# Down projections in 128 and 48 rows: two gated cross-attention layers with mixtures of experts

## The chip, the cores and the metric

The kernel runs on one core of a Trainium2 chip. The metric is the device time in microseconds (us) of one execution: the median of 3 runs of the kernel before is 1052.2 us (1050.12 to 1055.38). One more execution was taken with the hardware profiler; all rows below come from it.

The core has TensorE (PE, with PEld for its weight loads), VectorE (DVE), ScalarE (ACT), GpSimd (POOL) and SyncE (SP), which issues most DMAs.

## What is computed

2048 tokens of 256 numbers go through two layers. Each layer is a cross-attention to a context of 512 rows, then a feed-forward part: a shared network of inner width 704, and a mixture of experts (8 experts, the best 2 for each token in layer 0; 16 experts, the best 4 in layer 1) of inner width 176. The part that matters here, cut from the reference:

```python
h = silu(x @ gate_w.T) * (x @ up_w.T)        # [tokens, 176] of an expert, [tokens, 704] of the shared one
acc = acc + w[:, None] * (h @ down_w.T)      # back to 256 columns
shared = silu(x @ sgate.T) * (x @ sup.T) @ sdown.T
```

## The kernel before

**High and low halves.** All products of f32 numbers are made from f16 pairs: a number is a high f16 and a low f16 (what the high one leaves). A product is three matmuls, high x high, high x low and low x high (`HL`). The helper `mm3` (line 261) issues them for `C` = 2 pieces of the contraction, so six matmuls for one result of 128 rows. Most matmuls of the kernel therefore have line L261 in the trace; they are told apart by tiles and shapes.

**Experts.** Tokens are sorted into slots; a tile of 128 slots belongs to one expert, a group is two tiles. There are 20 groups in layer 0 and 40 in layer 1 (`NG`). `group(base, s)` is one round of a software pipeline, written once for each engine and run in a hardware loop of four rounds a turn, with the first four and the last few unrolled. In round s PE does, in this order: the four transposes of the gathered rows of group s+1 (L753), the gate and up matmuls of group s (L261, tiles `region` and `wkh`, 12 matmuls of 352 columns), the four transposes of h of group s-1 (L782), and the down matmuls of group s-2 (L261, 12 matmuls of 256 columns). h of a tile has 176 columns; they are cut into two pieces of `EC` = 88, so the transposed h fills 88 partitions of one PSUM bank (bank 6), [88, 512] for two tiles and two pieces.

ACT in the same round makes the high half of the inputs of group s+1 (L830), silu of group s (L839) and the high half of the transposed h of group s-1 (L843). DVE makes the low half of the inputs (L910) and two small operations for the routing weight, the product h of group s (L926, twice), the low half of the transposed h of group s-1 (L932), and copies the result of group s-2 out of PSUM (L937). SP stores that result; POOL gathers the rows of a group four rounds ahead with two indirect DMAs (L663), and may issue them when h of an earlier group is made. In every case what PE takes from ACT and DVE was asked for a round before, except the result of a transpose, which is asked for two rounds ahead.

**Weights.** Weights come as f32 through four staging buffers (`stg`) and are split into high and low halves in `region` (experts) and `sgu`, `sdn` (shared). In layer 0 POOL does all splits (`split_on_pool`, L1584 to L1587); the layer 1 weights are split by POOL between its gathers in layer 0's expert stage, one of three parts after each group (`split_part`, L1468 to L1473), and by POOL and ACT during the attention (L1496 to L1505).

**Shared network.** The tokens are four blocks of 512; for each block the inner width is taken in six steps, five of 128 rows and a last one of 64 (`SREM`). A step is 12 gate/up matmuls of 512 columns (6 in the last step) and 12 down matmuls of 256 columns (L729, tiles `sdn` and `wkh`), the down matmuls two steps later. The first block runs beside the routing, before the experts; the other three run after them, beside DVE's combination of the experts' rows (L879), for which POOL gathers (L697).

Of the kernel before, what the change touches and what calls it, by code (L numbers as in the profile page):

```python
# [13 lines left out]
P = 128  # L14
D = 256
# [17 lines left out]
def gated_flamingo(nc, a, out):  # L33
# [8 lines left out]
    KT = CTX // P  # L42
    EI = a["dn0"].shape[1]
    EG = 2 * EI
    EC = EI // 2
    SI = a["sdn0"].shape[0]
    SG = 2 * SI
# [16 lines left out]
    with ExitStack() as ctx:  # L64
# [3 lines left out]
        def sem(name):  # L68
# [28 lines left out]
              region[:, 0:16 * 4 * EG].rearrange("p (e h c n) -> p e h c n", e=16, h=2, c=C))  # L97
        DN = (region[0:EC, half + 8 * 4 * EG:EXP_COLS].rearrange("p (e h c n) -> p e h c n", e=8, h=2, c=2),
              region[0:EC, 16 * 4 * EG:EXP_COLS].rearrange("p (e h c n) -> p e h c n", e=16, h=2, c=2))
        sgu = sb("sgu", [P, 2, C, SG], F16)  # L100
# [604 lines left out]
        def sums_ahead(l):  # L705

            return 2 if l == 1 else 1

        def ffn_pe(pe, l):
            def shared_gate_up(s):  # L710
# [8 lines left out]
            def shared_down(s):  # L719

                k, v = s % KSH, s % HR
                r = P if k < SFULL else SREM
                at_least(pe, s_hl[l], 0, s + 1)
                if k == 0:
                    at_least(pe, s_accr[l], 0, s // KSH + 1 - sums_ahead(l))
                first = shared_sums(l, s)
                for i in range(4):
                    for n, (h, j) in enumerate(HL):
                        last = nc.tensor.matmul(PS[:, first + i // 2, i % 2 * D:(i % 2 + 1) * D],  # L729
                                                wkh[0:r, HR * h + v, i * P:(i + 1) * P],  # L730
                                                sdn[0:r, j, k, :], start=(k == 0 and n == 0 and i % 2 == 0),
                                                stop=(k == KSH - 1 and n == 2), skip_group_check=True)
                last.then_inc(s_d[l].sem, 1)
# [30 lines left out]
            def group(base, s):  # L764
# [13 lines left out]
                if inside(base, s, 1, NG[l] + 1):  # L778
                    at_least(pe, e_h[l], base, s)
                    for n in range(2):  # L780
                        for c in range(C):
                            last = nc.tensor.transpose(PS[0:EC, 6, (2 * n + c) * P:(2 * n + c + 1) * P],  # L782
                                                       wk1[:, 3 - u, n * EI + c * EC:n * EI + (c + 1) * EC], idf[:, :])
                    last.then_inc(e_hT[l].sem, 1)
                if inside(base, s, 2, NG[l] + 2):
                    e = experts(base, s - 2)
                    at_least(pe, e_y[l], base, s - 2)
                    for n in range(2):
                        last = mm3(PS[:, 7, n * D:(n + 1) * D],
                                   lambda i, c: wkh[0:EC, 4 + 2 * u + i, (2 * n + c) * P:(2 * n + c + 1) * P],  # L790
                                   lambda h, c: DN[l][:, bass.ds(e[n], 1), h, c, :].rearrange("p o n -> p (o n)"))
                    last.then_inc(e_d[l].sem, 1)
# [13 lines left out]
        def ffn_act(act, l):  # L806
# [25 lines left out]
            def group(base, s):  # L832
# [8 lines left out]
                if inside(base, s, 1, NG[l] + 1):  # L841
                    at_least(act, e_hT[l], base, s)
                    nc.scalar.activation(wkh[0:EC, 6 - 2 * u, :], PS[0:EC, 6, :], ACT.Copy).then_inc(e_hh[l].sem, 1)  # L843
            at_least(act, s_d[l], 0, HALF)
# [11 lines left out]
        def ffn_dve(dve, l):  # L856
# [36 lines left out]
            def shared_low(s):  # L893
                u, r = s % 2, (P if s % KSH < SFULL else SREM)
                at_least(dve, s_hh[l], 0, s + 1)
                at_least(dve, s_d[l], 0, s + 1 - HR)
                nc.vector.tensor_tensor(wkh[0:r, HR + s % HR, :], wk1[0:r, 2 + u, :], wkh[0:r, s % HR, :],  # L897
                                        ALU.subtract).then_inc(s_hl[l].sem, 1)
# [20 lines left out]
            def group(base, s):  # L919
# [508 lines left out]
        items += gu1[:GU_EARLY]  # L1428
        items += [(EC, a["dn1"][e].rearrange("(c p) n -> p c n", c=2), DN[1][:, e, 0], DN[1][:, e, 1]) for e in range(E[1])]
        items += gu1[GU_EARLY:]  # L1430
# [9 lines left out]
        items.append((SREM, a["sdn1"][SFULL * P:, :].unsqueeze(1), sdn[0:SREM, 0, SFULL:SFULL + 1, :], sdn[0:SREM, 1, SFULL:SFULL + 1, :]))  # L1440
        ROUNDS0 = 2 + E[0] // 2
# [75 lines left out]
        def _(sp):  # L1517
# [73 lines left out]
        def split_layer0(pl):  # L1591
# [15 lines left out]
        def split_experts0(pl, first, end):  # L1607
            for e in range(first, end):
# [3 lines left out]
                split_on_pool(pl, 2 * k + 1, seen, 2 * D, DN[0][:, e, 0].rearrange("p c n -> p (c n)"),  # L1612
                              DN[0][:, e, 1].rearrange("p c n -> p (c n)"), EC)
            if end == E[0]:
# [521 lines left out]
def laid_out(inputs):  # L2136

    import numpy as np
    v = {k: np.asarray(a) for k, a in inputs.items()}
    n = {}  # L2140
    n["x"] = v["x"].reshape(-1, v["x"].shape[-1])
# [5 lines left out]
    n["gu0"] = np.concatenate([v["L0_ffn_w_gate"], v["L0_ffn_w_up"]], 2)  # L2147
    n["dn0"] = v["L0_ffn_w_down"]
    n["gu1"] = np.concatenate([v["L1_ffn_gate_w"].transpose(0, 2, 1), v["L1_ffn_up_w"].transpose(0, 2, 1)], 2)
    n["dn1"] = v["L1_ffn_down_w"].transpose(0, 2, 1)  # L2150
    for l, (g, u, d) in enumerate(((v["L0_ffn_sw_gate"], v["L0_ffn_sw_up"], v["L0_ffn_sw_down"]),
                                   (v["L1_ffn_shared_gate_w"].T, v["L1_ffn_shared_up_w"].T, v["L1_ffn_shared_down_w"].T))):
        cuts = range(0, g.shape[1], 128)
        n[f"sgu{l}"] = np.concatenate([w[:, c:c + 128] for c in cuts for w in (g, u)], 1)
        n[f"sdn{l}"] = d
    n["g_xattn"], n["g_ffn"] = v["g_xattn"], v["g_ffn"]
# [21 lines left out]
```

## Time and profile before

| | |
|---|---|
| median of 3 runs | 1052.2 us (1050.12 to 1055.38) |
| span of the profiled execution | 1057.0 us, the only time known of it |
| mean granted TensorE clock | 0.824 of 2.4 GHz |
| PE, DVE, POOL, ACT busy | 859.4, 747.4, 627.5, 471.7 us |
| layer 0: first shared block, experts, rest of the shared network | about 150 to 190, 190 to 281, 281 to 360 us |
| layer 1 attention | about 360 to 700 us |
| layer 1: routing and first shared block, experts, rest | about 700 to 760, 761 to 946, 946 to 1057 us |

An instruction's row has its start, its duration, its engine and line (L12 is line 12 of the kernel), the tiles it writes and reads, and its shape. For matmuls `88*128` is the shape of the stationary tile, rows times columns, and `128x256` what comes out. The duration of a matmul includes its way through the array, so successive ones overlap; their pace is read from the differences of starts. The time in square brackets is what the engine was idle before the row and what ended it.

### The profile page before, as it was taken

How to read it: one execution, taken by the hardware profiler on the slowest of the kernel's cores; microseconds unless marked ns; L12 is line 12 of the kernel's file. 1: busy time of each engine (PE TensorE's matmuls, PEld its weight loads, DVE VectorE, ACT ScalarE, POOL GpSimd, SP SyncE). 2: the span in 40 equal slices, each digit the busy share in tenths (PEclk: the TensorE clock that was granted, in tenths of full speed). 3: DMA queues.
4: the chain of work that ended last, by engine and by line, in shares of the span. 5: the costliest groups of instructions: out<-in, count | busy, mean ns of one | idle time of the engine just before them, and what ended most of it. 6: DMA issues, size and time to landing. Idle time of an engine off the chain costs nothing.

```text
span 1057.0 us, 21171 instructions
## 1 busy us (share of the span) xinstructions
PE 859.4 (81%) x6928; PEld 579.0 (55%) x6929; DVE 747.4 (71%) x1624; ACT 471.7 (45%) x1018; POOL 627.5 (59%) x830
## 2 busy tenths in 40 slices
PE   4489668799988879887887787858699999879585
PEld 2267545577645446555555555544567788645243
DVE  5788768466566788898798888958666777536255
ACT  3455344233222368767667767734133334213111
POOL 4587882766284868878778788710244444624670
PEclk8689869899999955667668668868799999969787
DMA  7021242345231231121110100020134444432331
GB/s 255 21 83 29 62 133 60 111 137 151 98 109 49 81 130 38 62 95 43 61 43 15 29 26 4 2 71 16 33 108 130 126 140 133 136 96 71 104 95 50
DMA packets 65766, 85.55 MB, mean 81 GB/s; under 512 B 11148, under 2 KB 56976, under 8 KB 65680
## 3 DMA queue, kind: packets, MB, share of 16 engines
q1 hardware_dynamic: 55312, 55.30, 16.0%
q0 software_dynamic: 10368, 29.14, 10.4%
q8 instruction: 48, 0.79, 0.3%
q14 instruction: 38, 0.31, 0.1%
HBM read 61.93 MB, written 32.98 MB: 90 GB/s over the span
## 4 chain that ended last, share of the span: by engine, by line
PE 43%; DVE 16%; POOL 12%; issue 11%; POOLq 5%; DVEq 4%; ACT 4%; another core or an unknown queue 3%; DMA 2%; SPq 0%; ACTq 0%
PE PS L261 25%; PE PS L729 4%; DVE sb_slotv L1364 4%; POOL sb_xnf L663 3%; PE PS L753 2%; PE PS L782 2%; PE PS L1245 2%; DVE sb_wkh L1369 2%; PE PS L1235 1%; PE PS L370 1%; DMA sb_x_sb<-x 1%; PE PS L268 1%; PE PS L397 1%; POOL sb_wk L1703 1%
## 5 line engine op out<-in xcount | busy, mean ns | idle before, releaser
L261 PE MATMUL PS<-sb_region,sb_wkh 88*128 (+1 forms) x1440 | 213.4, 299 | 13.0 <-issue 9.4
L663 POOL DMA_INDIRECT sb_xnf<-token_table,sb_ids x120 | 115.9, 966 | 166.6 <-DVE sb_ids L577 75.0
L1364 DVE TENSOR_REDUCE sb_slotv<-PS 128x1 f32<-128x512 f32 x256 | 163.7, 681 | 26.5 <-PE PS L1235 26.5
L261 PEld LDWEIGHTS PS<-sb_region,sb_wkh 88*128 88x128 f16 (+1 forms) x1440 | 140.6, 100 | 63.3 <-issue 18.8
L261 PE MATMUL PS<-sb_xnT,sb_sgu 128*128 128x512 f16 x528 | 136.3, 407 | 12.7 <-issue 11.9
L811 ACT ACTIVATE sb_wk<-PS 128x512 f32<-128x512 f32 (+1 forms) x48 | 28.6, 595 | 172.2 <-PE PS L261 131.4
L1319 ACT ACTIVATE sb_wk<-PS,sb_slotv 128x512 f32<-128x512 f32 x128 | 87.1, 690 | 23.8 <-DVE sb_slotv L1364 23.5
L261 PEld LDWEIGHTS PS<-sb_xnT,sb_sgu 128*128 128x128 f16 x528 | 53.0, 103 | 80.5 <-issue 33.2
L729 PE MATMUL PS<-sb_sdn,sb_wkh 128*128 128x256 f16 (+1 forms) x576 | 76.5, 284 | 22.1 <-DVE sb_wkh L897 13.5
L1703 POOL TENSOR_SCALAR sb_wk<-sb_wk 128x512 f32<-128x512 f32 x128 | 79.4, 620 | 16.6 <-ACT sb_wk L1319 7.1
L890 DVE SCALAR_TENSOR_TENSOR sb_wk<-PS,sb_wk 128x512 f32<-128x512 f32 (+1 forms) x48 | 33.2, 692 | 70.1 <-ACT sb_wk L811 56.3
L1369 DVE TENSOR_SCALAR sb_wkh<-PS 128x1024 f16<-128x1024 f16 x112 | 76.6, 684 | 8.4 <-PE PS L1257 8.4
L729 PEld LDWEIGHTS PS<-sb_sdn,sb_wkh 128*128 128x128 f16 (+1 forms) x576 | 56.4, 101 | 46.2 <-DVE sb_wkh L897 20.9
L926 DVE SCALAR_TENSOR_TENSOR sb_wk<-PS,sb_sm,sb_wk 128x176 f32<-128x176 f32 x120 | 42.6, 397 | 53.8 <-ACT sb_wk L839 47.0
L830 ACT ACTIVATE sb_wkh<-PS 128x512 f16<-128x512 f32 x60 | 35.8, 596 | 99.2 <-PE PS L753 67.2
L697 POOL DMA_INDIRECT sb_xnf<-slot_table,sb_place x48 | 46.8, 976 | 45.6 <-DMA slot_table<-sb_wa 17.1
L839 ACT ACTIVATE sb_wk<-PS 128x352 f32<-128x352 f32 x60 | 27.8, 463 | 89.8 <-PE PS L261 82.1
L910 DVE TENSOR_TENSOR sb_wkh<-PS,sb_wkh 128x512 f16<-128x512 f32 x60 | 41.4, 690 | 32.7 <-ACT sb_wkh L830 23.1
L1319 ACT ACTIVATE sb_wkh<-PS,sb_slotv 128x512 f32<-128x512 f32 x64 | 43.4, 683 | 33.6 <-DVE sb_slotv L1364 23.3
L753 PE MATMUL PS<-sb_idf,sb_xnf 128*128 128x128 f32 x240 | 39.4, 287 | 18.9 <-DMA sb_xnf<-token_table,sb_ids 16.9
L1245 PE MATMUL PS<-sb_idh,sb_wk 128*128 128x128 f16 x512 | 53.5, 264 | 1.2 <-POOL sb_wk L1703 0.7
L1245 PEld LDWEIGHTS PS<-sb_idh,sb_wk 128*128 128x128 f16 x512 | 38.9, 119 | 24.8 <-issue 22.7
(292 smaller groups left out, 1883.4 us busy)
## 6 DMA issues: line engine op xcount, KB each, us to landing
slot_table<-sb_wa SPq DMA_DIRECT2D x60, 256.0 KB
slot_table<-token_table SPq DMA_DIRECT2D x16, 640.0 KB
sb_stg<-gu SPq DMA_DIRECT2D x24, 352.0 KB, 3.0
sb_stg<-dn SPq DMA_DIRECT2D x24, 176.0 KB
token_table<-sb_xnf SPq DMA_DIRECT2D x16, 256.0 KB, 3.9
sb_stg<-sgu SPq DMA_DIRECT2D x8, 352.0 KB, 6.6
sb_x_sb<-x SPq DMA_DIRECT2D x1, 2048.0 KB, 12.1
out<-sb_x_sb SPq DMA_DIRECT2D x16, 128.0 KB
```

The lines of the kernel that those rows point to most:

```text
L261: last = nc.tensor.matmul(out_, lhs(i, c), rhs(j, c), start=(c == 0 and n == 0 and not begun), stop=(c == C - 1 and n == 2 and not more))
L663: nc.gpsimd.indirect_dma_start(xg[l][:, 2 * (g % XR) + n, :], None, xw[l][:, :], bass.IndirectOffsetOnAxis(ap=ids[:, 2 * g + n:2 * g + n + ...
L697: nc.gpsimd.indirect_dma_start(yr[l][r][:, k, :], None, ys[l][:, :], bass.IndirectOffsetOnAxis(ap=place[:, k, t:t + 1], axis=0))\
L729: last = nc.tensor.matmul(PS[:, first + i // 2, i % 2 * D:(i % 2 + 1) * D], wkh[0:r, HR * h + v, i * P:(i + 1) * P], sdn[0:r, j, k, :], st ...
L753: last = nc.tensor.transpose(PS[:, 4 + s % 2, (2 * n + c) * P:(2 * n + c + 1) * P], xg[l][:, 2 * (s % XR) + n, c * P:(c + 1) * P], idf[:, :])
L910: nc.vector.tensor_tensor(wkh[:, 2 * (s % 2) + 1, :], PS[:, 4 + s % 2, :], wkh[:, 2 * (s % 2), :], ALU.subtract).then_inc(e_xl[l].sem, 1)
L926: last = nc.vector.scalar_tensor_tensor(wk1[:, 2 + u, n * EI:(n + 1) * EI], PS[:, 2 * u + n, EI:EG], wv[u][:, n:n + 1], wk1[:, u, n * EI:( ...
L1245: last = nc.tensor.transpose(bank[:, (h * KT + k) * P:(h * KT + k + 1) * P], h_p[s % NE][:, h, k * P:(k + 1) * P], idh[:, :])
L1319: nc.scalar.activation(h_e[s % NE][:, h, :], PS[:, 2 * u + h, :], ACT.Exp, bias=h_nb[u][:, h:h + 1], accum_out=o_sum[v][:, head:head + 1]) ...
L1364: nc.vector.tensor_reduce(h_nb[u][:, h:h + 1], PS[:, 2 * u + h, :], AX, ALU.max, negate=True).then_inc(h_max, 1)
L1369: nc.vector.tensor_scalar(h_T[s % 2], PS[:, 4 + s % 2, :].bitcast(F16), -RB, None, ALU.add).then_inc(h_pc_dve, 1)
L1703: nc.gpsimd.tensor_scalar(h_e[s % NE][:, h], h_e[s % NE][:, h], 255.0, MAGIC + RB_BITS, ALU.mult, ALU.add).then_inc(h_int, 1)
```

## The change

The 176 inner columns of h are cut into 128 and 48 (`EREM`) instead of 88 and 88. The first piece needs three matmuls as before. Of the second, the high half is written to partitions 0 to 47 and the low half to partitions 64 to 111 of the same tile, and the down weights of this piece are laid out twice, at rows 0 to 47 and 64 to 111 with zeros between. One matmul over 112 rows then gives high x high and low x high, one more over the 48 high rows gives high x low weights: five matmuls in place of six for each tile (`DOWN_PARTS`). The transposes of h make [128, 128] and [48, 128] results, ACT's copy and DVE's subtraction become two instructions each, and a memset clears the partitions between 48 and 64. The shared network's last 64 rows are treated the same way: their low half goes to partitions 64 to 127, `sdn`'s last rows are laid out twice, and its last step has two matmuls in place of three for each of four results. The host lays the weights out (`down_parts`); DMAs and splits of these weights now have 128 rows.

```diff
+        LOW_AT = P // 2
+        DOWN_PARTS = ((P, 0, 0, 0), (P, 0, 0, 1), (P, 1, 0, 0), (LOW_AT + EREM, 0, 1, 0), (EREM, 0, 1, 1))
...
                 for i in range(4):
-                    for n, (h, j) in enumerate(HL):
+                    for n, (h, j) in enumerate(HL if k < SFULL else HL[:2]):
+                        r = P if k < SFULL or n == 0 else SREM
                         last = nc.tensor.matmul(PS[:, first + i // 2, i % 2 * D:(i % 2 + 1) * D],
                                                 wkh[0:r, HR * h + v, i * P:(i + 1) * P],
...
                     for n in range(2):
                         for c in range(C):
-                            last = nc.tensor.transpose(PS[0:EC, 6, (2 * n + c) * P:(2 * n + c + 1) * P],
-                                                       wk1[:, 3 - u, n * EI + c * EC:n * EI + (c + 1) * EC], idf[:, :])
+                            r = P if c == 0 else EREM
+                            last = nc.tensor.transpose(PS[0:r, 6, (2 * c + n) * P:(2 * c + n + 1) * P],
+                                                       wk1[:, 3 - u, n * EI + c * P:n * EI + c * P + r], idf[:, :])
...
                     for n in range(2):
-                        last = mm3(PS[:, 7, n * D:(n + 1) * D],
-                                   lambda i, c: wkh[0:EC, 4 + 2 * u + i, (2 * n + c) * P:(2 * n + c + 1) * P],
-                                   lambda h, c: DN[l][:, bass.ds(e[n], 1), h, c, :].rearrange("p o n -> p (o n)"))
+                        for p, (r, i, c, h) in enumerate(DOWN_PARTS):
+                            last = nc.tensor.matmul(PS[:, 7, n * D:(n + 1) * D],
+                                                    wkh[0:r, 4 + 2 * u + i, (2 * c + n) * P:(2 * c + n + 1) * P],
+                                                    DN[l][0:r, bass.ds(e[n], 1), h, c, :].rearrange("p o n -> p (o n)"),
+                                                    start=(p == 0), stop=(p == len(DOWN_PARTS) - 1))
...
-                    nc.scalar.activation(wkh[0:EC, 6 - 2 * u, :], PS[0:EC, 6, :], ACT.Copy).then_inc(e_hh[l].sem, 1)
+                    nc.scalar.activation(wkh[:, 6 - 2 * u, 0:2 * P], PS[:, 6, 0:2 * P], ACT.Copy)
+                    nc.scalar.activation(wkh[0:EREM, 6 - 2 * u, 2 * P:4 * P], PS[0:EREM, 6, 2 * P:4 * P],
+                                         ACT.Copy).then_inc(e_hh[l].sem, 1)
...
-                nc.vector.tensor_tensor(wkh[0:r, HR + s % HR, :], wk1[0:r, 2 + u, :], wkh[0:r, s % HR, :],
+                low = wkh[:, HR + s % HR, :] if r == P else wkh[SREM:2 * SREM, s % HR, :]
+                nc.vector.tensor_tensor(low, wk1[0:r, 2 + u, :], wkh[0:r, s % HR, :],
                                         ALU.subtract).then_inc(s_hl[l].sem, 1)
...
-                    nc.vector.tensor_tensor(wkh[0:EC, 7 - 2 * u, :], PS[0:EC, 6, :], wkh[0:EC, 6 - 2 * u, :],
-                                            ALU.subtract).then_inc(e_hl[l].sem, 1)
+                    nc.vector.tensor_tensor(wkh[:, 7 - 2 * u, 0:2 * P], PS[:, 6, 0:2 * P], wkh[:, 6 - 2 * u, 0:2 * P],
+                                            ALU.subtract)
+                    nc.vector.tensor_tensor(wkh[LOW_AT:LOW_AT + EREM, 6 - 2 * u, 2 * P:4 * P], PS[0:EREM, 6, 2 * P:4 * P],
+                                            wkh[0:EREM, 6 - 2 * u, 2 * P:4 * P], ALU.subtract).then_inc(e_hl[l].sem, 1)
...
+            nc.vector.memset(wkh[LOW_AT - 32:LOW_AT, 4::2, 2 * P:4 * P], 0.0)
             dve.drain()
...
-                    load(2 * k + 1, (base, 2 + s), de.rearrange("(c p) n -> p c n", c=2), 2 * D, EC)
+                    load(2 * k + 1, (base, 2 + s), de.rearrange("(c p) n -> p c n", c=2), 2 * D)
...
-            split_on_pool(pl, 3, 32, D, sdn[0:SREM, 0, SFULL, :], sdn[0:SREM, 1, SFULL, :], SREM)
+            split_on_pool(pl, 3, 32, D, sdn[:, 0, SFULL, :], sdn[:, 1, SFULL, :])
...
+    def down_parts(w):
+
+        rest = w[:, 128:]
+        gap = np.zeros((w.shape[0], 64 - rest.shape[1], w.shape[2]), w.dtype)
+        return np.concatenate([w[:, 0:128], rest, gap, rest, gap], 1)
```

## Rows read from the trace of the kernel before

**Rows 1.** The page: engines' busy time, and the chain by line.
```profile
PE 859.4 (81%) x6928; PEld 579.0 (55%) x6929; DVE 747.4 (71%) x1624; ACT 471.7 (45%) x1018; POOL 627.5 (59%) x830
...
PE PS L261 25%; PE PS L729 4%; DVE sb_slotv L1364 4%; POOL sb_xnf L663 3%; PE PS L753 2%; PE PS L782 2%; PE PS L1245 2%; DVE sb_wkh L1369 2%; PE PS L1235 1%; PE PS L370 1%; DMA sb_x_sb<-x 1%; PE PS L268 1%; PE PS L397 1%; POOL sb_wk L1703 1
```

**Rows 2.** Windows: busy us (x) of PE, PEld, DVE, ACT, POOL; granted clock; DMA share, GB/s.
```profile
191.00:281.00 90.00, 84.26 (x634) 64.29 (x633) 56.60 (x136) 31.32 (x59) 51.60 (x52) 0.96 0.44 130
771.00:915.00 144.00, 141.63 (x1120) 111.39 (x1119) 102.17 (x246) 55.52 (x106) 68.36 (x75) 1.00 0.45 131
```

**Rows 3.** The timeline, PE alone, one round of layer 1's experts.
```profile
863.49 0.60 PE L753 MATMUL PS<-sb_idf,sb_xnf 128*128 128x128 f32 x4
863.93 1.95 PE L261 MATMUL PS<-sb_region,sb_wkh 128*128 x12
865.72 0.60 PE L782 MATMUL PS<-sb_idf,sb_wk 128*88 128x128 f32 x4
866.15 1.48 PE L261 MATMUL PS<-sb_region,sb_wkh 88*128 x12
867.47 0.60 PE L753 MATMUL PS<-sb_idf,sb_xnf 128*128 128x128 f32 x4
```

**Rows 4.** The chain that ended last, 183 to 282 us: shares by line, and splits.
```profile
by line: POOL sb_xnf L663 25.6%; issue 21.0%; PE PS L261 20.3%; DMA sb_xnf<-token_table,sb_ids 6.8%; POOL sb_region L1473 6.1%; POOLq L1472 5.1%; POOL sb_stg L1470 3.1%; POOL sb_region L1468 3.1%; PE PS L753 2.7%; PE PS L782 2.4%; DVE sb_wk
...
200.81 1.52 POOL sb_region L1473
...
213.71 1.52 POOL sb_region L1473
```

**Rows 5.** The timeline, PE alone, layer 0's experts, where it waited.
```profile
207.50 0.90 PE L753 MATMUL PS<-sb_idf,sb_xnf 128*128 128x128 f32 x4 [2.24 <-DMA sb_xnf<-token_table,sb_ids]
208.45 3.29 PE L261 MATMUL PS<-sb_region,sb_wkh 128*128 x12
...
234.24 0.66 PE L753 MATMUL PS<-sb_idf,sb_xnf 128*128 128x128 f32 x4 [0.86 <-DMA sb_xnf<-token_table,sb_ids]
```

**Rows 6.** The timeline, PE alone, shared steps of layer 1.
```profile
968.85 2.75 PE L261 MATMUL PS<-sb_xnT,sb_sgu 128*128 128x512 f16 x12
971.44 1.47 PE L729 MATMUL PS<-sb_sdn,sb_wkh 128*128 128x256 f16 x12
972.75 2.75 PE L261 MATMUL PS<-sb_xnT,sb_sgu 128*128 128x512 f16 x12
975.44 1.48 PE L729 MATMUL PS<-sb_sdn,sb_wkh 64*128 64x256 f16 x12
976.85 2.76 PE L261 MATMUL PS<-sb_xnT,sb_sgu 128*128 128x512 f16 x12
```

**Rows 7.** The timeline, weight loads alone, at the same step.
```profile
975.43 0.55 PEld L729 LDWEIGHTS PS<-sb_sdn,sb_wkh 64*128 64x128 f16 x6 [0.42 <-issue]
```

**Rows 8.** The timeline, PE alone, bias rows of one row.
```profile
54.47 0.39 PE L268 MATMUL PS<-sb_lg,sb_ones_h 1*128 1x256 f16 x2
54.79 0.83 PE L261 MATMUL PS<-sb_wa,sb_wkh 128*128 128x256 f16 x6
55.55 0.39 PE L268 MATMUL PS<-sb_lg,sb_ones_h 1*128 1x256 f16 x2
```

**Rows 9.** Groups by line and shape: count, busy us, mean ns, idle before.
```profile
L843 ACT ACTIVATE sb_wkh<-PS 88x512 f16<-88x512 f32 x60 | 35.4, 590 | 9.4 <-PE PS L782 7.5 <-remote 1.7
L839 ACT ACTIVATE sb_wk<-PS 128x352 f32<-128x352 f32 x60 | 27.8, 463 | 89.8 <-PE PS L261 82.1 <-issue 5.4 <-remote 2.4
L926 DVE SCALAR_TENSOR_TENSOR sb_wk<-PS,sb_sm,sb_wk 128x176 f32<-128x176 f32 x120 | 42.6, 397 | 53.8 <-ACT sb_wk L839 47.0 <-issue 6.7
L932 DVE TENSOR_TENSOR sb_wkh<-PS,sb_wkh 88x512 f16<-88x512 f32 x60 | 40.8, 679 | 5.8 <-ACT sb_wkh L843 2.8 <-issue 2.4
```

**Rows 10.** The same view, POOL alone, low halves of weights.
```profile
L1505 POOL TENSOR_TENSOR sb_region<-sb_stg,sb_region 88x512 f16<-88x512 f32 x14 | 16.1, 1151 | 2.3 <-issue 2.3
L1505 POOL TENSOR_TENSOR sb_sdn<-sb_stg,sb_sdn 128x512 f16<-128x512 f32 x2 | 2.3, 1156 | 0.3 <-issue 0.3
```

More of the change, by code:

```diff
@@ L42, in gated_flamingo @@
     KT = CTX // P
[L43 to L46, printed above, removed]
+    EG = a["gu0"].shape[2]
+    EI = EG // 2
+    EREM = EI - P
+    SI = a["sgu0"].shape[1] // 2
     SG = 2 * SI
@@ L97, in gated_flamingo @@
               region[:, 0:16 * 4 * EG].rearrange("p (e h c n) -> p e h c n", e=16, h=2, c=C))
-        DN = (region[0:EC, half + 8 * 4 * EG:EXP_COLS].rearrange("p (e h c n) -> p e h c n", e=8, h=2, c=2),
-              region[0:EC, 16 * 4 * EG:EXP_COLS].rearrange("p (e h c n) -> p e h c n", e=16, h=2, c=2))
+        DN = (region[:, half + 8 * 4 * EG:EXP_COLS].rearrange("p (e h c n) -> p e h c n", e=8, h=2, c=2),
+              region[:, 16 * 4 * EG:EXP_COLS].rearrange("p (e h c n) -> p e h c n", e=16, h=2, c=2))
         sgu = sb("sgu", [P, 2, C, SG], F16)
@@ L721, in shared_down @@
                 k, v = s % KSH, s % HR
-                r = P if k < SFULL else SREM
                 at_least(pe, s_hl[l], 0, s + 1)
@@ L731, in shared_down @@
                                                 sdn[0:r, j, k, :], start=(k == 0 and n == 0 and i % 2 == 0),
-                                                stop=(k == KSH - 1 and n == 2), skip_group_check=True)
+                                                stop=(k == KSH - 1 and n == 1), skip_group_check=True)
                 last.then_inc(s_d[l].sem, 1)
@@ L1428, in gated_flamingo @@
         items += gu1[:GU_EARLY]
-        items += [(EC, a["dn1"][e].rearrange("(c p) n -> p c n", c=2), DN[1][:, e, 0], DN[1][:, e, 1]) for e in range(E[1])]
+        items += [(P, a["dn1"][e].rearrange("(c p) n -> p c n", c=2), DN[1][:, e, 0], DN[1][:, e, 1]) for e in range(E[1])]
         items += gu1[GU_EARLY:]
@@ L1439, in gated_flamingo @@
             items.append((P, g[:, cs, :], sdn[:, 0, cs, :], sdn[:, 1, cs, :]))
-        items.append((SREM, a["sdn1"][SFULL * P:, :].unsqueeze(1), sdn[0:SREM, 0, SFULL:SFULL + 1, :], sdn[0:SREM, 1, SFULL:SFULL + 1, :]))
+        items.append((P, a["sdn1"][SFULL * P:, :].unsqueeze(1), sdn[:, 0, SFULL:SFULL + 1, :], sdn[:, 1, SFULL:SFULL + 1, :]))
         ROUNDS0 = 2 + E[0] // 2
@@ L1552, in _ @@
                 load(n, (0, 1), d[:, cs, :], (cs.stop - cs.start) * D)
-            load(3, (0, 1), a["sdn0"][SFULL * P:, :].unsqueeze(1), D, SREM)
+            load(3, (0, 1), a["sdn0"][SFULL * P:, :].unsqueeze(1), D)
             def two_experts(base, s):
@@ L1612, in split_experts0 @@
                 split_on_pool(pl, 2 * k + 1, seen, 2 * D, DN[0][:, e, 0].rearrange("p c n -> p (c n)"),
-                              DN[0][:, e, 1].rearrange("p c n -> p (c n)"), EC)
+                              DN[0][:, e, 1].rearrange("p c n -> p (c n)"))
             if end == E[0]:
@@ L2147, in laid_out @@
     n["gu0"] = np.concatenate([v["L0_ffn_w_gate"], v["L0_ffn_w_up"]], 2)
-    n["dn0"] = v["L0_ffn_w_down"]
+    n["dn0"] = down_parts(v["L0_ffn_w_down"])
     n["gu1"] = np.concatenate([v["L1_ffn_gate_w"].transpose(0, 2, 1), v["L1_ffn_up_w"].transpose(0, 2, 1)], 2)
-    n["dn1"] = v["L1_ffn_down_w"].transpose(0, 2, 1)
+    n["dn1"] = down_parts(v["L1_ffn_down_w"].transpose(0, 2, 1))
     for l, (g, u, d) in enumerate(((v["L0_ffn_sw_gate"], v["L0_ffn_sw_up"], v["L0_ffn_sw_down"]),
@@ L2154, in laid_out @@
         n[f"sgu{l}"] = np.concatenate([w[:, c:c + 128] for c in cuts for w in (g, u)], 1)
-        n[f"sdn{l}"] = d
+        n[f"sdn{l}"] = np.concatenate([d, d[len(d) // 128 * 128:]], 0)
     n["g_xattn"], n["g_ffn"] = v["g_xattn"], v["g_ffn"]
```

## The prediction, made before the change was built or run

> **What bounds the kernel now.** I read the page's busy shares and its chain first. PE is busy 81% of the span and its matmul line L261 alone is 25% of the chain, but POOL, DVE and idle "issue" time hold much of the rest [rows 1]. So the change has to be priced stage by stage, and I went to the table of windows for the two expert stages. In layer 1's (771 to 915 us) PE is busy 141.6 of 144 us at full granted clock, DVE 102, POOL 68 and ACT 56 [rows 2]: PE sets the pace. In layer 0's (191 to 281 us) PE is busy 84 of 90 us.
>
> The timeline of PE in layer 1 shows one round [rows 3]: four input transposes (L753) from 863.49, twelve gate/up matmuls from 863.93, four h transposes (L782) from 865.72, twelve down matmuls (88 rows) from 866.15, the next transposes at 867.47. That is 0.44 + 1.79 + 0.43 + 1.32 = 3.98 us, nothing between them. A down matmul costs 1.31 / 12 = 0.109 us, a transpose the same. Everything else in a round depends on the round before, so what PE needs per round is what the stage costs, forty times.
>
> Layer 0's twenty rounds are different. The chain there is mostly POOL's gathers and weight splits [rows 4]. POOL serves three groups from one L1473 to the next, 213.71 - 200.81 = 12.9 us on the shortest turn: 4.30 us a group, 0.3 more than PE's 3.98. PE therefore stands waiting for gathers three times, 3.9 us in all; the first two stand in [rows 5], 2.24 and 0.86.
>
> **What the change takes away.** Each group has 10 down matmuls in place of 12: 2 x 0.109 = 0.22 us a round. The shared network's last step of each block of 512 tokens has 8 matmuls in place of 12: 0.44 us, four blocks in each layer. The down matmuls with 88 rows and the shared ones with 128 both start 0.109 us apart [rows 3, 6], so filling the rows costs nothing by itself.
>
> **What it adds on PE.** The shapes now alternate. Of the ten down matmuls the fifth and the tenth have a stationary tile of 48 rows, the others of 128 or 112. Of the four h transposes the second and the fourth have 48 columns (the loop still runs n outside, c inside). In a shared last step 128 and 64 rows alternate four times. The trace has such a border: the shared step with 64 rows, between steps with 128 [rows 6]. The gate/up matmuls ahead of it take 975.44 - 972.75 = 2.69 us, where those ahead of a 128-row step take 971.44 - 968.85 = 2.59; the 64-row step itself takes 976.85 - 975.44 = 1.41 us, where a 128-row one takes 1.31. So entering costs 0.10 us and leaving costs 0.10 us. The weight-load row says how: the first load of the 64-row tile comes after 0.42 us without one [rows 7], while loads otherwise run ahead of the matmuls. Bias rows of one row show the same: two matmuls take 54.79 - 54.47 = 0.32 us in place of 0.22, and six matmuls after them 0.76 in place of 0.65 [rows 8]. 88 rows pay nothing, 64 and 1 row pay; 48 lies between the two that pay, so I count 48 rows as paying.
>
> The Trainium skill, "TensorEngine Tiling (Array Packing)", section "Key Properties", says that changing the tiling mode, not just the tile, drains TensorE; its list of row modes steps from 128 to 64 to 32 rows. The trace agrees for rows, with 0.10 us each way. By this rule the change trades 0.22 us of matmuls for the borders.
>
> Down matmuls: into and out of 48 rows twice, 4 x 0.10 = 0.40, less 0.22: +0.18 us a round. Transposes: into and out of 48 columns twice. No row of the trace has fewer than 88 columns, so the price of a column border is bounded from below by 0 (88 columns pay nothing) and from above by 0.10 plus a doubled transpose. I take 0.10, the price of the only change of shape the trace shows: 4 x 0.10 = +0.40 us. Together a round costs 3.98 + 0.58 = 4.56 us.
>
> **What it adds elsewhere.** ACT's copy of h becomes two. 352 columns take 0.463 us and 512 take 0.590 [rows 9], 0.8 ns a column, so two of 256 take about 0.78: +0.19. DVE's subtraction becomes two: by its 176-column and 512-column rows (0.397 and 0.679 us), 0.46 each, +0.25 at most. DVE is busy 2.8 us of a 3.98 us round and ACT 1.5 [rows 2], and PE asks for the result one round later, so both are hidden; only where the pipeline empties at a layer's end do they show, some 0.35 us twice, 0.7 in all. If PE were not the bound they would cost 0.2 each a round. POOL's splits run over 128 rows in place of 88 at the same 512 columns: 1151 ns with 88 rows, 1156 with 128 [rows 10]: nothing, and so for the shared last rows. The loads of down weights grow from 176 to 256 KB; they are issued ahead and POOL stands between their landing and their use, nothing, and 0.5 us each on the few first ones if not. One memset of DVE per layer falls where DVE waits for gathers: nothing, else 0.4. Its new waits: none; the semaphore of each pair is on the second instruction.
>
> **The sum.** Layer 1: of 40 rounds, 36 lie in the full stretch (144 / 3.98), the others where the pipeline fills and empties and PE waits in part, which absorbs some. I take 38 x 0.58 = 22.0 us (34 to 40 rounds: 19.7 to 23.2). Layer 0: 20 x 0.58 = 11.6, but with 4.56 us PE is now slower than POOL's 4.30, so the three waits (3.9 us) go and with them most of the half-clock group behind the first (3.29 in place of 1.95 us [rows 5], 1.3): +6.4 (5 to 11.6). Shared last steps: six more borders, 0.60, less 0.44: +0.16, eight times: +1.3 (0 to 1.5). Ends: +0.7. In all +30.4 us. The profiled execution has a span of 1057.0 us, 4.8 over the median of the runs, 1052.2; it goes to 1087, the median to **1082**. With the bounds, and some 3 us for the stages behind, where work meets other work when it is shifted, this case by itself gives 1072 to 1093.
>
> **Rivals.**
> *Column borders are free.* Speaks for it: nothing in the trace shows one. Then a round costs +0.18: 38 x 0.18 = 6.8, in layer 0 the round of 4.16 stays under POOL's 4.30 and half of 3.6 shows, 1.8; with the shared steps and ends 10.6: 1063.
> *The 48-column transposes also get slower themselves.* A 128-column f32 transpose takes 0.109 us, twice what 128 f16 columns could take at the rate of 256 in 0.109 [rows 3, 6]; f32 goes at half rate already, and if a narrow tile halves it once more, two of four transposes double: +0.22 a round, 58 times, 12.7 us: 1095. The Trainium skill, "TensorEngine Tiling (Array Packing)", section "Restrictions", lists the f32 transpose mode among what column tiling disables; no row here shows it.
> *No borders at all: faster.* If tiles of 48 rows and of 48 columns are handled as the 88-row ones are, the change does what it removes: -0.22 x 38 = -8.3 in layer 1; in layer 0 PE carries the chain in only some 9 rounds, -2.0; the shared steps -0.44 x 8 = -3.5 if 64-row matmuls too alternate freely; ends +0.7: 1039. The deciding point is whether a border costs over 0.22 / 4 = 0.055 us in the down part. The 64-row and 1-row rows speak against it.
> *DVE becomes the bound* would need its 2.8 us plus 0.25 to pass PE's round; it doesn't in any case above.
>
> **How the numbers follow.** Borders on both: 0.62. Columns free: 0.14. Slower transposes as well: 0.11. No borders: 0.10. The 0.03 left is a net of nothing. The predicted time is the first case's, 1082. The range goes from 1058 (columns free, with some cover) to 1098; it leaves out the case without borders and little above. Half a per cent is 5.3 us, about what a measurement can tell from no change: faster 0.10, same 0.04, slower 0.86.
>
> **What would show it.** In layer 1 the round should be 4.56 us: gate/up still 1.79, the h transposes 0.8 in place of 0.43, the down part 1.5 in place of 1.32. Matmuls of 48 rows should start about 0.2 us after the one before and be followed after 0.2. In layer 0 the waits of PE for gathers should be gone. A round of 4.16 with transposes at 0.43 would mean free columns; one of 3.76 would overturn the argument; one near 4.8 would mean slower transposes. PE idle between rounds, waiting for DVE or ACT, would mean that the cover failed.

## The result, and the profile after

The changed kernel takes 1058.17 us, median of 20 runs (1054.2 to 1065.17), where the kernel before, run beside it, takes 1051.77 (1046.4 to 1057.88, 20 runs). The ratio is 1.0064, 95% interval 1.0043 to 1.0084: slower by 6.4 us, where 30 had been forecast. The span of its profiled execution is 1059.6 us. Medians here and below are of all runs; the ratios leave out the slow ones, those over 1.5% above the fastest run of the same kernel.

The page: busy time by engine, and the chain that ended last by line (L794 are the down matmuls of the experts, L732 those of the shared network, L756 and L786 the transposes).

```profile
PE 868.5 (82%) x6776; PEld 558.3 (53%) x6777; DVE 761.1 (72%) x1686; ACT 475.0 (45%) x1078; POOL 630.3 (59%) x830
...
PE PS L261 20%; PE PS L794 7%; DVE sb_slotv L1376 4%; PE PS L732 4%; PE PS L756 3%; PE PS L786 2%; PE PS L1257 2%; DVE sb_wkh L1381 2%; PE PS L1247 1%; POOL sb_xnf L663 1%; PE PS L370 1%; POOL sb_wk L1715 1%; DMA sb_x_sb<-x 1%; PE PS L268 1%
```

Against [rows 1], PE has 152 matmuls fewer (6928 to 6776) and is busy 9 us more: fewer, but dearer. The same windows as [rows 2] (busy us and count of PE, PEld, DVE, ACT, POOL; granted clock; DMA share; GB/s):

```profile
191.00:281.00 90.00, 84.73 (x576) 56.96 (x576) 61.29 (x155) 32.29 (x78) 54.25 (x55) 0.96 0.43 130
771.00:915.00 144.00, 142.28 (x995) 97.21 (x994) 103.58 (x268) 54.48 (x134) 64.57 (x69) 0.98 0.41 123
```

In layer 1 PE is still busy nearly all the time (142.3 of 144 us), and DVE is no nearer to being the bound (103.6 of 144 us, 102.2 before). One round of this stage, the timeline of PE alone and then of its weight loads:

```profile
863.90 0.66 PE L756 MATMUL PS<-sb_idf,sb_xnf 128*128 128x128 f32 x4
864.39 1.95 PE L261 MATMUL PS<-sb_region,sb_wkh 128*128 x12
866.18 0.60 PE L786 MATMUL PS<-sb_idf,sb_wk 128*128 128x128 f32 x4
866.62 1.57 PE L794 MATMUL PS<-sb_region,sb_wkh 128*128 x10
868.12 0.66 PE L756 MATMUL PS<-sb_idf,sb_xnf 128*128 128x128 f32 x4
```

```profile
866.04 0.47 PEld L786 LDWEIGHTS PS<-sb_idf,sb_wk 128*128 128x128 f32 x4
866.51 0.43 PEld L794 LDWEIGHTS PS<-sb_region,sb_wkh 128*128 128x128 f16 x4
867.15 0.54 PEld L794 LDWEIGHTS PS<-sb_region,sb_wkh 48*128 48x128 f16 x5 [0.21 <-issue]
867.91 0.09 PEld L794 LDWEIGHTS PS<-sb_region,sb_wkh 48*128 48x128 f16 x1 [0.21 <-issue]
868.12 0.42 PEld L756 LDWEIGHTS PS<-sb_idf,sb_xnf 128*128 128x128 f32 x4
```

Against [rows 3] the parts stand so: input transposes 0.49 (0.44), gate and up 1.79 (1.79), h transposes 0.44 (0.43), down 1.50 (1.32). The round is 868.12 - 863.90 = 4.22 us, where 3.98 became 4.56 in the forecast. The h transposes, two of which now have 48 columns, take what they took. The loss is in the down part and in the step behind it (+0.18 and +0.05), beside the tiles of 48 rows. The load rows show where: in front of each of the two 48-row loads there is a hole of 0.21 us in which nothing is loaded, as there was one of 0.42 at the 64-row tile of [rows 7]; and the load for the next transposes comes at the time of their first matmul, 868.12, while the one for the h transposes is ahead of it (866.04 and 866.18).

The shared network's last step, the timeline of PE, to be held against [rows 6]:

```profile
978.78 1.47 PE L732 MATMUL PS<-sb_sdn,sb_wkh 128*128 128x256 f16 x12
980.09 2.75 PE L261 MATMUL PS<-sb_xnT,sb_sgu 128*128 128x512 f16 x12
982.68 1.77 PE L732 MATMUL PS<-sb_sdn,sb_wkh 128*128 128x256 f16 x8
984.38 2.76 PE L261 MATMUL PS<-sb_xnT,sb_sgu 128*128 128x512 f16 x12
```

Eight matmuls take 984.38 - 982.68 = 1.70 us, where twelve took 1.41; the gate and up matmuls before them take 2.59 in place of 2.69, for the first tile behind them now has 128 rows. Together that is +0.19 us a block.

ACT's two copies of the transposed h and DVE's two subtractions (by line and shape: count, busy us, mean ns, idle before), the rows that answer to L843 and L932 of [rows 9]:

```profile
L849 ACT ACTIVATE sb_wkh<-PS 128x256 f16<-128x256 f32 x60 | 23.0, 383 | 6.0 <-PE PS L786 2.7 <-remote 1.7 <-issue 1.6
L850 ACT ACTIVATE sb_wkh<-PS 48x256 f16<-48x256 f32 x60 | 21.9, 365 | 0.0
L943 DVE TENSOR_TENSOR sb_wkh<-PS,sb_wkh 48x256 f16<-48x256 f32 x60 | 25.1, 418 | 0.8
L941 DVE TENSOR_TENSOR sb_wkh<-PS,sb_wkh 128x256 f16<-128x256 f32 x60 | 24.9, 415 | 3.2 <-issue 2.3 <-ACT sb_wkh L850 0.7
```

0.75 us in place of 0.59, and 0.83 in place of 0.68: +0.16 and +0.15, both hidden in the round.

What is left to explain: 40 + 20 rounds at +0.24 and eight blocks at +0.19 are 15.9 us if nothing absorbs them, and the kernel lost 6.4. Besides, the last stage of the profiled executions (from the second shared gate/up matmuls to the last shared down matmul) is 97.5 us long after, and 104.7 before, as if the change gave 7 us back there.

### The profile page after: what moved, and what is told of

Its sections match the earlier page's. It is cut to its first block, busy times and chain, and to the rows that moved or that the text cites. A ratio compares the mean times of both kernels' runs of the same rounds, so it can differ in the third digit from the quotient of the medians.

```text
span 1059.6 us, 20989 instructions
## 1 busy us (share of the span) xinstructions
PE 868.5 (82%) x6776; PEld 558.3 (53%) x6777; DVE 761.1 (72%) x1686; ACT 475.0 (45%) x1078; POOL 630.3 (59%) x830
## 4 chain that ended last, share of the span: by engine, by line
PE 46%; DVE 15%; POOL 10%; issue 10%; POOLq 5%; DVEq 4%; ACT 4%; another core or an unknown queue 4%; DMA 2%; SPq 0%; ACTq 0%
PE PS L261 20%; PE PS L794 7%; DVE sb_slotv L1376 4%; PE PS L732 4%; PE PS L756 3%; PE PS L786 2%; PE PS L1257 2%; DVE sb_wkh L1381 2%; PE PS L1247 1%; POOL sb_xnf L663 1%; PE PS L370 1%; POOL sb_wk L1715 1%; DMA sb_x_sb<-x 1%; PE PS L268 1%
## 5 line engine op out<-in xcount | busy, mean ns | idle before, releaser
L261 PE MATMUL PS<-sb_xnT,sb_sgu 128*128 128x512 f16 x528 | 130.8, 397 | 7.9 <-issue 7.2
L261 PE MATMUL PS<-sb_region,sb_wkh 128*128 x720 | 123.2, 321 | 7.9 <-issue 7.8
L794 PE MATMUL PS<-sb_region,sb_wkh 128*128 x600 | 95.0, 277 | 4.4 <-DVE sb_wa L948 4.1
L732 PE MATMUL PS<-sb_sdn,sb_wkh 128*128 128x256 f16 (+1 forms) x544 | 77.0, 283 | 24.7 <-DVE sb_wkh L906 15.0
L261 PEld LDWEIGHTS PS<-sb_region,sb_wkh 128*128 128x128 f16 x720 | 71.7, 100 | 44.6 <-issue 10.7
L732 PEld LDWEIGHTS PS<-sb_sdn,sb_wkh 128*128 128x128 f16 (+1 forms) x544 | 53.3, 100 | 52.1 <-DVE sb_wkh L906 21.8
L794 PEld LDWEIGHTS PS<-sb_region,sb_wkh 128*128 128x128 f16 x600 | 52.6, 97 | 43.2 <-issue 32.1
L756 PE MATMUL PS<-sb_idf,sb_xnf 128*128 128x128 f32 x240 | 41.4, 298 | 15.3 <-DMA sb_xnf<-token_table,sb_ids 15.3
```

The costliest lines, as they stand in the source:

```text
L261: last = nc.tensor.matmul(out_, lhs(i, c), rhs(j, c), start=(c == 0 and n == 0 and not begun), stop=(c == C - 1 and n == 2 and not more))
L756: last = nc.tensor.transpose(PS[:, 4 + s % 2, (2 * n + c) * P:(2 * n + c + 1) * P], xg[l][:, 2 * (s % XR) + n, c * P:(c + 1) * P], idf[:, :])
L794: last = nc.tensor.matmul(PS[:, 7, n * D:(n + 1) * D], wkh[0:r, 4 + 2 * u + i, (2 * c + n) * P:(2 * c + n + 1) * P], DN[l][0:r, bass.ds(e[ ...
```

## The experiments

**Full rows.** The last down matmul of a tile goes over 112 rows like the one before it, and that of the shared network over 128. The weights are laid out twice anyway, so this adds the product low x low of the short piece, which all the other sums leave out; it takes nothing away. No tile of fewer than 112 rows is left. The column widths of the h transposes still alternate.

```diff
-        DOWN_PARTS = ((P, 0, 0, 0), (P, 0, 0, 1), (P, 1, 0, 0), (LOW_AT + EREM, 0, 1, 0), (EREM, 0, 1, 1))
+        DOWN_PARTS = ((P, 0, 0, 0), (P, 0, 0, 1), (P, 1, 0, 0), (LOW_AT + EREM, 0, 1, 0), (LOW_AT + EREM, 0, 1, 1))
...
-                        r = P if k < SFULL or n == 0 else SREM
+                        r = P
```

> The changed kernel with the last matmul of the down product, and the last of the shared step, over all rows of their stationary tile (112 and 128 in place of 48 and 64): the same number of matmuls, no matmul with 48 rows left, and 64-row tiles only where the kernel before the change has them outside these steps. The products added are low x low, so the sum is the same product, a little more exact. Theory: the cost is the borders between tiles of 128 and of 64 rows, and they alone. Then a round of layer 1's experts goes from 4.22 to 3.98 - 0.22 = 3.76 us, the expert stage of layer 1 is 38 x 0.22 = 8 us shorter than before the change and 18 us shorter than with it, and the kernel is 5 to 12 us faster than before the change. Rival: the cost is in the doubled copies of ACT and DVE, or in the weights' layout: the round stays at 4.2 us. Second rival: DVE becomes the bound: a round of 3.9 or more with PE waiting for DVE.

Measured: 1042.81 us (1039.84 to 1044.71, 6 runs) beside 1054.7 of the kernel before (23 runs); ratio 0.9896, interval 0.9855 to 0.9936. The timeline of PE:

```profile
851.71 0.60 PE L756 MATMUL PS<-sb_idf,sb_xnf 128*128 128x128 f32 x4
852.15 1.95 PE L261 MATMUL PS<-sb_region,sb_wkh 128*128 x12
853.94 0.60 PE L786 MATMUL PS<-sb_idf,sb_wk 128*128 128x128 f32 x4
854.38 1.26 PE L794 MATMUL PS<-sb_region,sb_wkh 128*128 x10
855.48 0.60 PE L756 MATMUL PS<-sb_idf,sb_xnf 128*128 128x128 f32 x4
```

The round is 3.77 us: 0.44 + 1.79 + 0.44 + 1.10, ten down matmuls at 0.110. So the same ten matmuls, with no tile of 48 rows, cost 4.22 - 3.77 = 0.45 us less; that is 0.11 for each of four borders. And the transposes of 48 columns stand between those of 128 as before and cost nothing. The theory held for the round and for the time (11.9 us under the kernel before, 5 to 12 forecast), and this version beats both kernels. The whole stage gained less than the 18 us forecast against the changed kernel: from its first expert matmul to the shared network behind it, it takes 173.3 us, where the changed kernel has 184.0 to 186.3 in its three profiles and the kernel before 180.8 to 186.7.

**48-row tiles side by side.** The second token tile of a group takes its parts in the opposite order, so the two 48-row matmuls stand together; so too in the shared step. Borders: two a round in place of four.

```diff
-                        for p, (r, i, c, h) in enumerate(DOWN_PARTS):
+                        for p, (r, i, c, h) in enumerate(DOWN_PARTS if n == 0 else DOWN_PARTS[::-1]):
```

> The changed kernel with the second tile's five matmuls in reverse order, so that the two 48-row matmuls of a group stand side by side, and likewise the 64-row matmuls of each pair of results in the shared step: two borders in and out per group in place of four. Theory: each border costs 0.115 us (a quarter of 4.22 - 3.76), so the round is 3.76 + 2 x 0.115 = 3.99 us, level with the kernel before the change, and the time is within 3 us of before. Rival (the price belongs to each 48-row matmul and not to the border): the round stays at 4.2 us.

Measured: 1048.41 us (1041.06 to 1058.36, 12 runs) beside 1054.7, ratio 0.9935, interval 0.9903 to 0.9967. PE:

```profile
851.95 0.60 PE L756 MATMUL PS<-sb_idf,sb_xnf 128*128 128x128 f32 x4
...
854.62 1.47 PE L794 MATMUL PS<-sb_region,sb_wkh 128*128 x10
855.92 0.60 PE L756 MATMUL PS<-sb_idf,sb_xnf 128*128 128x128 f32 x4
```

A round of 3.97 us, between 3.77 and 4.22: two borders cost 0.20, four 0.45. What counts is how often the rows change, not how many matmuls are short. The time was to be within 3 us of before and is 6 under it. Two things that the forecast left out go that way: a shared last step and the gate and up matmuls before it now take 3.88 us together, 0.22 less than before the change, eight times; and layer 1's rounds have no pauses here, which the kernel before mostly has (the table below).

**Borders alone.** In the kernel before, the last of the six down matmuls of each tile runs over 64 rows of 88; the contributions of the other 24 rows to that product are left out. No matmul is added or removed.

```diff
+        SHORT = (5,)
...
+                            r = 64 if p in SHORT else EC
```

> The kernel before the change with the last of the six down matmuls of each tile over 64 of its 88 rows (24 rows of one of the small products are left out): the same count of matmuls, copies and transfers, but four borders a group. Theory: the round of layer 1's experts goes from 3.98 to 3.98 + 4 x 0.115 = 4.44 us, layer 1's stage gets 17 us longer, layer 0's some 5, and the whole is 15 to 24 us slower. Rival (the number of rows of a tile is free and the price in the changed kernel comes from elsewhere): the round stays at 3.98 us.

Measured: 1074.55 us, one run, 20 over the 1054.7 of the kernel before; 15 to 24 were forecast. PE:

```profile
855.31 1.95 PE L261 MATMUL PS<-sb_region,sb_wkh 128*128 x12
857.10 0.60 PE L784 MATMUL PS<-sb_idf,sb_wk 128*88 128x128 f32 x4
857.54 1.79 PE L794 MATMUL PS<-sb_region,sb_wkh 88*128 x12
859.26 0.66 PE L755 MATMUL PS<-sb_idf,sb_xnf 128*128 128x128 f32 x4
859.75 0.46 PE L261 MATMUL PS<-sb_region,sb_wkh 128*128 x2
```

The round is 859.75 - 855.31 = 4.44 us, 0.46 over the 3.98 of [rows 3], 0.115 a border. The border's price doesn't come with the changed layout, and a tile of 64 rows pays as one of 48 does.

**Was the last stage shortened by the change?** In both kernels PE stops several times there while POOL issues its gathers, in part waiting for nothing that the profile shows. One thought was that the place of an instruction in PE's stream decides when PE stops, and that the change's fewer matmuls move it. Two kernels move the stream without other work: PE gets waits that are already met, between layer 1's attention and its routing, 120 of them in the kernel before and 136 in the changed one.

```diff
             attn1_pe(pe)
+            for _ in range(120):
+                pe.wait_ge(const_ready, 1)
             route_pe(pe, 1)
```

> The kernel before the change with 120 waits that are already met, put into PE's program between the attention and the routing of layer 1, where PE waits for other engines anyway. The work is the same. In the profile of the changed kernel the last stage (rest of the shared network, beside POOL's gathers) is 97.5 us, before the change it is 104.7 us, with the same number of gathers, and PE stops in it at places some 256 instructions apart while the gathers run. The changed kernel's program for PE is about 136 instructions shorter up to there; 120 = 256 - 136 put the same places into the same position. Theory: where these stops fall decides how long the last stage is, so here it is 97 to 99 us and the kernel is 4 to 7 us faster than before. Rival: the last stage is shorter because it starts later against something else (POOL's gathers, PE's clock): then it stays at 104 to 106 us and the time within 1 us of before.

Measured: 1053.52 us (1049.65 to 1063.58, 12 runs), ratio 0.9994, interval 0.9959 to 1.0028. The 4 to 7 us did not come.

> The changed kernel with 136 waits that are already met in PE's program between the attention and the routing of layer 1, so that the last stage's instructions stand, counted in blocks of 256, where they stand before the change. In six profiles so far the last stage is shorter the later the second stop of PE begins before POOL's last gather: 9, 7, 7, 4, 4 and 3 us ahead give 104.7, 100.1, 100.2, 97.4, 96.7 and 97.5 us. Theory: moving the stops earlier costs here: stage 100 us or more, kernel 2 to 5 us slower than the changed kernel, so 0.8 to 1.1% slower than before. Rival: position is worth nothing in the medians: within 1 us of the changed kernel, 0.6% slower than before.

Measured: 1059.15 us (1049.96 to 1070.05, 12 runs) beside 1053.58, ratio to the kernel before 1.0042, interval 1.0 to 1.0084; the changed kernel without the waits has 1.0064. So neither kernel's time depends on that place by more than a measurement can tell. Nor did the stops move: the changed kernel's long one stands before the 219th matmul behind the experts in both of its profiles and in the one with 136 waits. (The traces show only 59 of the 120 waits and 67 of the 136, so how far the stream was moved is not certain.) What the two don't settle is the last stage itself, since one profile each shows it. So both kernels were profiled once more, unchanged:

> The kernel before the change, nothing altered: a second profile. If its last stage is 104 to 105 us again, the 7 us by which the changed kernel's is shorter belong to the change; if it is near 100, the first profile was an unlucky one and 3 us remain. The stretch up to the first shared matmul (153.8 us before, 156.7 in the changed kernel) should differ by up to 3 us between two profiles of the same kernel.

> The changed kernel, nothing altered: a second profile, beside the one of the kernel before. The round of layer 1's experts is 4.22 us again; the last stage 97 to 98 us if its length belongs to the kernel, elsewhere between 96 and 105 if it belongs to the execution.

The executions took 1052.81 and 1054.87 us, and the changed kernel's round was 4.22 us again. The stretch up to the first shared matmul is 155.4 and 152.1 us, where the first profiles had 153.8 and 156.7: two executions of the changed kernel differ there by 4.6 us and not by up to 3. The windows of the last stage, in this order: the kernel before, the kernel before again, the changed kernel, the changed kernel again:

```profile
946.90:1051.60 104.70, 82.52 (x414) 42.07 (x414) 52.19 (x93) 19.94 (x36) 49.16 (x48) 0.81 0.27 78
```
```profile
947.60:1045.60 98.00, 75.99 (x414) 41.09 (x414) 52.16 (x93) 20.04 (x36) 49.13 (x48) 0.86 0.29 84
```
```profile
956.70:1054.20 97.50, 75.57 (x402) 39.60 (x402) 52.61 (x93) 19.94 (x36) 49.77 (x48) 0.88 0.29 84
```
```profile
945.40:1047.70 102.30, 75.40 (x402) 40.85 (x402) 52.63 (x93) 19.93 (x36) 48.78 (x48) 0.87 0.28 80
```

The kernel before takes 104.7 and 98.0, the changed one 97.5 and 102.3; with 120 and 136 more waits it is 100.1 and 98.9, against forecasts of 97 to 99 and of 100 or more. The order has turned round: these profiles show no 7 us that belong to the change; two executions of one kernel differ by as much.

**Half of the gathers.** What does PE stop for? This kernel is the one before the change, but POOL gathers two of the four expert rows of each token in layer 1, and DVE adds those two twice; the other two rows are left out of the result.

```diff
-                gather_rows(pl, 1, t, (3, 2, 1))
+                gather_rows(pl, 1, t, (1,))
...
-                gather_rows(pl, 1, t)
+                gather_rows(pl, 1, t, (0, 1))
```

> The kernel before the change, with two of the four gathers of each token tile in layer 1's last stage (half of the experts' results are left out of the sum; VectorE's additions are kept at the same number and size). PE's work is the same. Theory: what lengthens the last stage beyond PE's own 70 us are the stops of PE at places some 256 instructions apart while POOL's gathers run, and a stop lasts until the gathers pause or end. With 32 gathers the burst ends about 30 us earlier, the second stop disappears and the stage goes from 97 to 105 us to 80 to 88. Rival: PE's stops come from elsewhere (VectorE's order of work, the clock): the stage stays within 3 us of 100.

Measured: 1010.12 us, one run. The window of its last stage, and then PE's waits in the same stage of this kernel and of the kernel before:

```profile
931.90:1002.90 71.00, 68.89 (x414) 40.19 (x414) 52.29 (x93) 20.17 (x36) 25.83 (x24) 0.98 0.24 71
```
```profile
PE PS L729 <- DVE sb_wkh L897: 2.1, 2, 1.3
PE PS L261 <- issue: 0.3, 1, 0.3
```
```profile
PE PS L261 <- issue: 11.6, 14, 1.5
PE PS L729 <- DVE sb_wkh L897: 5.3, 4, 2.2
PE PS L729 <- issue: 5.2, 5, 1.9
```

PE does the same 414 matmuls in 71 us in place of 98 to 104.7, less than the 80 to 88 forecast. POOL's 48 gathers there became 24. The waits "<-issue", for nothing the profile shows, go from 16.8 us to 0.3, and the granted clock from 0.81 to 0.98. In the second profile of the kernel before they are only 7.9 us, and the stage is still 98 us long, because PE waits another 13.9 us for DVE there. DVE waits for ACT, and ACT starts long after its input is there. PE and ACT in that profile ("remote": the profile names nothing that ended the wait):

```profile
979.00 2.75 PE L261 MATMUL PS<-sb_xnT,sb_sgu 128*128 128x512 f16 x12
999.85 0.60 ACT L811 ACTIVATE sb_wk<-PS 128x512 f32<-128x512 f32 x1 [20.01 <-remote]
```

The silu (L811) of this step has its input from PE at 981.8 and starts 18.1 us later, 3.3 us after the end of a row of POOL's gathers. In each of the nine profiles with all gathers one silu of this stage starts 18 to 21 us after its input, and others up to 13 us after theirs; with half of the gathers all 18 start some 0.1 us after:

```profile
967.77 0.60 ACT L811 ACTIVATE sb_wk<-PS 128x512 f32<-128x512 f32 x1 [2.78 <-PE PS L261]
```

So ScalarE stops beside the gathers as TensorE does, and its stop is enough to hold PE: behind the step at 979.00 PE can do one more gate/up step, and then needs a low half (L897) that DVE makes after the product of the late silu. At full pace PE would have been there at about 985.6 (an estimate, 2.6 us from the start of that step at 983.0); the low half was begun at 1001.1. PE's own stops between the two cost nothing in this execution. The same happens at the end of the experts, where PE leaves its loop while POOL issues 12 + 4 gathers, here 4 + 4: PE waits there in the kernel before, and not at the same place in this one:

```profile
917.42 0.60 PE L782 MATMUL PS<-sb_idf,sb_wk 128*88 128x128 f32 x4
923.24 2.74 PE L261 MATMUL PS<-sb_region,sb_wkh 88*128 x12 [5.22 <-issue]
```
```profile
909.90 0.60 PE L782 MATMUL PS<-sb_idf,sb_wk 128*88 128x128 f32 x4
910.34 1.48 PE L261 MATMUL PS<-sb_region,sb_wkh 88*128 x12
```

So the stops of PE and of ACT go with the number of gathers that are under way. By what way a gather on POOL holds them up, and how much of the 27 us or more is the shorter gathering itself and not the stops, no run here separates.

## Why the prediction was right in direction and wrong in size

**What bounds the kernel: right.** PE's round sets the pace of layer 1's experts; the full rows took 0.45 us from the changed kernel's round, and 30 rounds became 126.6 - 115.7 = 10.9 us shorter, the kernel some 18 us (6.4 over the kernel before with the borders, 11.9 under it without, each beside its own runs of it).

**Row borders: right in kind, a little too cheap.** Put at 0.10 each from [rows 6]; they cost 0.10 (two a round, and in the shared step) to 0.115 (four a round), so a round pays +0.24 where +0.18 was forecast, a shared block +0.19 where +0.16 was. This was the deciding question (over 0.055 us or not), and the profile of before answered it. The Trainium skill, "TensorEngine Tiling (Array Packing)", section "Key Properties", says that a change of tiling mode drains TensorE; for rows the traces agree, with 0.10 to 0.115 us a border. The forecast that 48 rows pay like 64 held.

**Column borders: the step that failed.** The prediction says: "I take 0.10, the price of the only change of shape the trace shows: 4 x 0.10 = +0.40 us." It carried the price of a row border over to columns, and it was the largest term: 0.40 of 0.58 a round, some 15 of 22 us in layer 1 and most of layer 0's 6.4. The h transposes with 128 and 48 columns alternating take 0.44 us for four, as with 88. If a narrow stationary tile were a change of mode for columns as it is for rows, there would be a drain here too; nothing drains, and an f32 transpose of 48 columns takes no longer. The lower bound, 0, was the truth. The text had noted that nothing in the trace showed a column border, gave free columns a chance of 0.14, and worked that rival out to 1063. It was the mechanism; its time came out above the measured one because of the next two terms. That the measured 1058.2 lies inside the stated range, at its very end, is due to that end having been taken from this rival, "with some cover"; the main sum doesn't reach it. Its own bounds add up to some 1074 to 1092, a little less wide than the 1072 to 1093 given.

**Layer 1's rounds: another term was missing.** At +0.24, 38 rounds would be 9.1 us. The profiles give less. The time of 30 rounds in the middle of the stage, start to start of the h transposes:

| kernel | us | per round | the shortest rounds | pauses in all |
|---|---|---|---|---|
| before | 121.5 | 4.05 | 3.98 | 2.1 |
| before, again | 124.5 | 4.15 | 3.98 | 5.1 |
| before, 120 waits | 124.5 | 4.15 | 3.98 | 5.1 |
| before, half of the gathers behind | 119.3 | 3.98 | 3.98 | 0 |
| after; again; with 136 waits | 126.6 each | 4.22 | 4.22 | 0 |
| 48-row tiles side by side | 119.0 | 3.97 | 3.97 | 0 |
| full rows | 115.7 | 3.86 | 3.76 | 2.9 |

PE's round of 3.98 us was read from the second half of the stage, where it holds without a gap. In the first half, and all through in two other executions, it doesn't. The kernel before again, PE alone:

```profile
860.43 0.60 PE L753 MATMUL PS<-sb_idf,sb_xnf 128*128 128x128 f32 x4
860.92 1.96 PE L261 MATMUL PS<-sb_region,sb_wkh 128*128 x12
862.72 0.60 PE L782 MATMUL PS<-sb_idf,sb_wk 128*88 128x128 f32 x4
863.15 1.48 PE L261 MATMUL PS<-sb_region,sb_wkh 88*128 x12
864.47 0.60 PE L753 MATMUL PS<-sb_idf,sb_xnf 128*128 128x128 f32 x4
865.27 1.96 PE L261 MATMUL PS<-sb_region,sb_wkh 128*128 x12 [0.20 <-issue]
```

From transposes to gate/up it is 0.49 us in one round and 0.80 in the next, in place of 0.44. Such a longer step comes every fourth round, the length of one turn of the hardware loop; a turn takes some 16.6 us, 4.15 a round. In the changed kernel, with 30 matmuls in 4.22 us in place of 32 in 3.98, it doesn't occur in any of three executions. So the change pays 7 us in these 30 rounds (borders less saved matmuls) and saves 0 to 5 us of pauses; what is left is 126.6 less 119.3 to 124.5, 2 to 7 us, 4 in the mean of the four executions. The other rounds add nothing to it: the first 36 rounds of the stage take 148.4 us in the mean of three profiles before (one of them with the 120 waits) and 152.5 in the mean of three after (one with the 136), 4.1 more. That the loop's turn is late because PE's sequencer has too little lead is argued from this pattern and not shown; why one execution has none and another loses them half way stays open.

**Layer 0: the cover held.** From its first expert matmul to the shared network behind it: 90.2, 90.4 and 91.0 us before (with the 120 waits the last), 92.2, 92.0 and 91.1 after, about +1.2, where +6.4 was forecast and 1.8 by the rival. The stage goes by POOL and not by PE as long as PE's round is the shorter: with rounds of 3.76 and 3.97 it takes 90.3 and 89.9 us, and with 4.44 (borders alone) 95.1. The round of 4.22 is under POOL's 4.30 [rows 4], so PE still waits for gathers. In the changed kernel:

```profile
210.08 0.66 PE L756 MATMUL PS<-sb_idf,sb_xnf 128*128 128x128 f32 x4 [0.56 <-DMA sb_xnf<-token_table,sb_ids]
...
216.57 0.66 PE L756 MATMUL PS<-sb_idf,sb_xnf 128*128 128x128 f32 x4 [1.66 <-DMA sb_xnf<-token_table,sb_ids]
```

The forecast that these waits would be gone fell with the 4.56.

**The sum, as the runs show it.** Layer 1's rounds +4, layer 0 +1.2, eight shared steps 8 x 0.19 = +1.5: 7 us, with an uncertainty of some 2 us, since the first term is a mean over few executions; measured 6.4, interval 4.5 to 8.8 (0.43 and 0.84% of 1051.8). The ends of the layers (+0.7 forecast) are below what two executions differ by. ACT's and DVE's second instructions were priced at +0.19 and at most +0.25, and took 0.16 and 0.15, hidden; the wider loads and splits show nowhere.

**No borders at all,** the rival on the fast side, needed under 0.055 us a border. The full rows show what it was worth: it was put at 13 us under the kernel before, and that kernel is 11.9 under it. The gain was there, and the way to it was to remove the borders.

## What to carry to other kernels

At the full clock a matmul of 256 columns over 48, 64 or 88 rows cost as much here as one over 128, and more than that where it alternates tiles of 48 or 64 rows with larger ones: fill the short tile's rows with zeros or with products that are wanted anyway, or put the short ones next to each other. Price a border from a row that shows that very border; where the trace has none of the kind, the bounds are the answer, and a neighbour's price is no middle. And read a round's length over the whole stage and not from its cleanest stretch: what pauses are in it decides what a longer round costs.

## What was not expected of the hardware

- Going from a stationary tile of 112 or 128 rows to one of 48 or 64, or back, costs 0.10 to 0.115 us at full clock, while 88, 112 and 128 rows alternate freely (0.109 to 0.110 us a matmul), and 48 and 128 columns too, in f32 transposes at 0.11 us each.
- TensorE and ScalarE stop beside indirect gathers on POOL: one silu of the last stage starts 18 to 21 us after its input with 48 gathers, some 0.1 with 24; PE's "issue" waits are 16.8 and 7.9 us in two profiles with 48, 0.3 with 24, and the granted clock falls with the stops (0.81 and 0.86, 0.98 without). Halving the gathers, which leaves out half of the experts' rows, took 43 us from the kernel, more than any edit of the matmuls here.
- The same stage of the same kernel is 98.0 us long in one execution and 104.7 in another, while the spans differ by 6: a difference of that size between two single profiles of a stage is no finding.
